# Graph outputs and first feed-forward chunk: order of loads, clears, rows and splits changed

## The reference

```python
# graph attention, h = 4 heads; x is layer-normed
alpha = einsum(q[dst], k[src]) / sqrt(512); attn = softmax over the edges of dst
agg = segment_sum(attn * v[src], dst)
x_attn = agg + x @ Wskip + bskip
h = x_attn @ Wlin + blin + x_attn[:, :512]
x1 = x + gamma * (h - mean(h)) / sqrt(var(h) + 1e-5) + beta
# feed-forward on xf = layernorm(x1), e = 4 experts
weights = normalised(max(softmax(xf @ gate_w.T) - sigmoid(xf @ thr_w.T) / e, 0))
hidden = relu(einsum('ni,ehi->neh', xf, fc1_w))
lo = (hidden @ lora_A) @ lora_B; x2 = x1 + sum_e weights * (lo @ fc2_w)
# used later: the sum of edge_attr (64 columns) and the count of edges per dst
```

## Time and profile before

| what | value |
|---|---|
| device time, median of 3 | 1934.83 us (1934.49 to 1940.91) |
| the profiled execution's own time | 1933.92 us |
| its span | 1932.3 us |
| granted TensorE clock, mean | 0.963 |
| PE busy | 1773.4 us, 92% |
| DVE busy | 1309.0 us, 68% |
| ACT busy | 909.0 us, 47% |
| POOL busy | 587.7 us, 30% |
| output loop | about 759 to 943 us |
| first chunk | 957 to about 1040 us |

### The profile page before, as it was taken

The page is one execution under the profiler, slowest core; times in us unless marked ns, Lnnn a source line. Parts: engine busy times, 40 slices in busy tenths (PEclk is TensorE's granted clock), DMA queues, the critical chain, the costliest instruction groups (busy, mean ns, idle before and its releaser), DMA issues. The chain is left out here.

```text
span 1932.3 us, 31958 instructions
## 1 busy us (share of the span) xinstructions
PE 1773.4 (92%) x10958; PEld 1542.0 (80%) x10958; DVE 1309.0 (68%) x2957; ACT 909.0 (47%) x1655; POOL 587.7 (30%) x532
## 2 busy tenths in 40 slices
PE   7998999899999999888679999999899999999496
PEld 5776899788888888776568998988788888888385
DVE  5444466788888886466764566545588788886676
ACT  4332366677777775222231233324465555555321
POOL 0000102655555551001100112122254535443234
PEclk9999999899999999998889999999999999999698
DMA  6752677877777774656213038876021111203432
GB/s 242 215 187 83 201 257 247 224 204 198 203 202 202 204 201 122 162 126 157 84 49 110 1 110 149 203 214 194 11 43 23 43 32 32 43 23 125 155 121 88
DMA packets 183532, 265.14 MB, mean 137 GB/s; under 512 B 55852, under 2 KB 102443, under 8 KB 181109
## 3 DMA queue, kind: packets, MB, share of 16 engines
q1 hardware_dynamic: 117839, 169.58, 30.1%
q0 software_dynamic: 49920, 62.94, 12.2%
q10 hardware_dynamic: 15640, 30.90, 6.5%
HBM read 198.55 MB, written 85.86 MB: 147 GB/s over the span
## 5 line engine op out<-in xcount | busy, mean ns | idle before, releaser
L1092 POOL DMA_INDIRECT edge_rows<-xn_store,edge_index x200 | 242.5, 1213 | 170.1 <-PE psum L138 108.5
L2599 POOL TENSOR_TENSOR mprob<-mprob,mrden 125x1250 f32<-125x1250 f32 x80 | 181.6, 2271 | 219.6 <-DVE mrden L2705 219.1
L2628 ACT ACTIVATE mprob<-psum,mbias 125x1250 f32<-125x1250 f32 x80 | 104.3, 1303 | 152.4 <-DVE mbias L2714 152.4
L1310 DVE TENSOR_TENSOR edge_xt_lo<-psum,edge_xt_hi 128x500 fp32r<-128x500 f32 x200 | 134.8, 675 | 56.3 <-ACT edge_xt_hi L1185 56.3
L1185 ACT ACTIVATE edge_xt_hi<-psum 128x500 fp32r<-128x500 f32 x200 | 117.5, 589 | 91.6 <-PE psum L1485 91.6
L2712 DVE TENSOR_REDUCE mmin<-psum 125x1 f32<-125x512 f32 (+1 forms) x240 | 126.9, 584 | 46.6 <-PE psum L2871 46.3
L2889 PE MATMUL psum<-ident,mprob 125*125 125x125 f32 x800 | 117.9, 292 | 17.9 <-DVE ptm_lo L2719 9.8
L2889 PEld LDWEIGHTS psum<-ident,mprob 125*125 125x125 f32 x800 | 100.3, 191 | 35.5 <-DVE ptm_lo L2719 20.4
L2719 DVE TENSOR_TENSOR ptm_lo<-psum,ptm_hi 125x500 fp32r<-125x500 f32 (+1 forms) x240 | 126.4, 582 | 2.0 <-ACT ptm_hi L2634 2.0
L1485 PE MATMUL psum<-ident,edge_rows 125*128 125x125 f32 x800 | 119.7, 273 | 4.8 <-DVE edge_xt_lo L1310 2.5
L1339 DVE TENSOR_TENSOR edge_rows_lo<-edge_rows,edge_rows_hi 125x1024 fp32r<-125x1024 f32 x100 | 121.2, 1212 | 0.0
(11 more groups left out here) (519 smaller groups left out, 5364.1 us busy)
## 6 DMA issues: line engine op xcount, KB each, us to landing
slots_in<-blank_rows ACTq DMA_DIRECT2D x20, 1026.0 KB, 16.8
t_store<-t_part SPq DMA_DIRECT2D x20, 1000.0 KB, 5.4
t_row<-t_store SPq DMA_DIRECT2D x47, 400.0 KB, 6.8
y_store<-y_rows SPq DMA_DIRECT2D x50, 200.0 KB
q_chunk<-q_store SPq DMA_DIRECT2D x40, 250.0 KB, 5.6
y_tile<-y_store SPq DMA_DIRECT2D x10, 896.0 KB
edge_attr<-in_attr SPq DMA_DIRECT2D x50, 112.0 KB
moe_xg<-slots_in SPq DMA_DIRECT2D x17, 256.5 KB, 3.6
```

The costliest lines, as they stand in the source:

```text
L1092: nc.gpsimd.indirect_dma_start(xe[t % RING][:, s, :], None, g.xn_store, bass.IndirectOffsetOnAxis(ap=index[t % RING][:, s, 0:1], axis=0)). ...
L1310: nc.vector.tensor_tensor(xt_lo[:, k, :], x_bank(KT * t + k), f32(xt_hi[:, k, :]), ALU.subtract).then_inc(x_low, 1)
L2599: nc.gpsimd.tensor_tensor(prob[:, n % 4, :], prob[:, n % 4, :], rden[:, n % 4:n % 4 + 1].broadcast_to([P, N]), ALU.mult).then_inc(p_ready, 1)
```

## The change

In the output loop: the first base rows, beta and the last rows of x are issued inside SP's loop (t = 0 and t = 6) behind the edge features, and the wait for the y stores goes; `fin.xin` is loaded at step 9 instead of 5, and POOL adds beta 4 windows later, so that those windows' clears stand ahead of it; `bound`, `turn_f` and `pass_ranges` are written in turn 38; some semaphores (`turn_inner`) are cleared ahead of the wait for `pass_done`. `scale` also writes `shift2`, minus mean times scale. In the first chunk: ACT writes rows 4 to 7 from `shift2` and `r2`; POOL's first clear waits for the four rows of DVE; the last pair's results follow its centring, with each later step one place earlier; ACT splits expert 3's weights behind `first_hi(8)` and `first_hi(9)`; DVE's `b_pads` comes earlier and its part of that split between the gates' spans; PE takes `second(0)` ahead of the last turns and the gates.

```diff
...
@@ -689,10 +689,12 @@
                                   [x[:, k, a:b] for x in xt], k == 0, k == KT - 1)
             last.then_inc(self.wide, 1)
 
-    def vector_rows(self, nc, dve):
+    def vector_rows(self, nc, dve, between=None):
         for q, (a, b) in enumerate(SPANS):
             dve.wait_ge(self.wide, q + 1)
             last = nc.vector.tensor_copy(self.rows[:, a:b], self.core.bank(q)[0:self.ROWS, 0:b - a])
+            if between is not None and q + 1 < len(SPANS):
+                between(q)
...
+        self.shift2 = at("fin_shift2", [P, NT], F32, 3.75)
...
     def scale(self, nc, link, c):
 
         rough_root(nc, link, self.r0[:], self.ve[:], self.h[:], (12.0, 768.0))
-        link(nc.vector.tensor_scalar(self.r2[:, 2 * c:2 * c + 2], self.r0[:], ROOT_SCALE, None, ALU.mult))
+        pair = slice(2 * c, 2 * c + 2)
+        link(nc.vector.tensor_scalar(self.r2[:, pair], self.r0[:], ROOT_SCALE, None, ALU.mult))
+        return nc.vector.scalar_tensor_tensor(self.shift2[:, pair], self.mv2[:, pair, 0], -1.0, self.r2[:, pair], ALU.mult, ALU.mult)
...
-    edge_inner, inner = [], []
+    edge_inner, turn_inner, inner = [], [], []
...
+    def turn_sem(name):
+        turn_inner.append(sem(name))
+        return turn_inner[-1]
+
...
-    attr_in, attr_top, attr_low = [loop_sem(f"attr_in{i}") for i in range(ATTRS)], loop_sem("attr_top"), loop_sem("attr_low")
-    hot_clear, hot_ready, agg_done, agg_out = (loop_sem(n) for n in ("hot_clear", "hot_ready", "agg_done", "agg_out"))
+    attr_in, attr_top, attr_low = [turn_sem(f"attr_in{i}") for i in range(ATTRS)], turn_sem("attr_top"), loop_sem("attr_low")
+    hot_clear, hot_ready, agg_done, agg_out = (turn_sem("hot_clear"), *(loop_sem(n) for n in ("hot_ready", "agg_done", "agg_out")))
...
 
@@ -1022,17 +1031,17 @@
                     if t == 1:
                         y_load(1)
                 y_store(WINDOWS - 1)
-                sp.dma_start(fin.beta[:], row_view(w["beta"])).then_inc(xin_in, 16)
-                in_two(sp, fin.last_xin[:], pair(w["x"], FIN), xin_in)
-                for i in range(2):
-                    sp.wait_ge(y_stored[i], 16 * (WINDOWS // 2))
-                in_two(sp, g.acc[:, 0:2, :], pair(g.base_store, 0), base_in)
                 for t in range(WINDOWS):
                     if t + RING < WINDOWS:
                         sp.wait_ge(hot_ready, t + 1)
                         firsts.append(index_load(sp, t + RING, index_in[t % RING]))
                     if t + ATTRS < WINDOWS:
                         attr_load(t + ATTRS, firsts[t + ATTRS])
+                    if t == 0:
+                        in_two(sp, g.acc[:, 0:2, :], pair(g.base_store, 0), base_in)
+                    if t == 6:
+                        sp.dma_start(fin.beta[:], row_view(w["beta"])).then_inc(xin_in, 16)
+                        in_two(sp, fin.last_xin[:], pair(w["x"], FIN), xin_in)
                     if t == 3:
                         for s in edge_inner:
                             sp.sem_clear(s)
@@ -1049,12 +1058,14 @@
                     if step == 1 and c:
                         sp.wait_ge(o_added, 2 * c)
                         in_two(sp, pair(g.base_store, c - 1), g.acc[:, 2 * c - 2:2 * c, :], base_out)
-                    if step == 5 and c < FIN:
+                    if step == 9 and c < FIN:
                         if c:
                             sp.wait_ge(xin_used, 2 * c)
                         in_two(sp, fin.xin[:], pair(w["x"], c), xin_in)
                 sp.wait_ge(o_added, NT)
                 in_two(sp, pair(g.base_store, FIN), g.acc[:, 2 * FIN:, :], base_out)
+                for s in turn_inner:
+                    sp.sem_clear(s)
                 sp.wait_ge(pass_done, 4 * turn + 4)
                 sp.sem_inc(pass_over, 1)
                 for s in inner:
@@ -1132,8 +1143,8 @@
                     nc.gpsimd.memset(f32(hot[i][:]), 0.0).then_inc(hot_clear, 1)
                 for t in range(WINDOWS):
                     clear(t)
-                    c, step = divmod(t, 2 * PER_TILE)
-                    if step == 9 and c < FIN:
+                    c, step = divmod(t - 4, 2 * PER_TILE)
+                    if step == 9 and 0 <= c < FIN:
                         pool.wait_ge(xin_in, 32 * c + 16 + 64)
                         nc.gpsimd.tensor_tensor(fin.xin[:], fin.xin[:], bc(fin.beta[:], 2), ALU.add).then_inc(xin_ready, 1)
                 nc.gpsimd.tensor_tensor(fin.last_xin[:], fin.last_xin[:], bc(fin.beta[:], 2), ALU.add).then_inc(xin_ready, 1)
...
                 if step == 15:
-                    fin.scale(nc, link, c)
+                    link(fin.scale(nc, link, c))
...
@@ -1442,11 +1453,12 @@
                     if h == 0 and r:
                         add_out(r - 1)
                         edge_sums(r - 1)
+                    if n == TURNS - 2:
+                        nc.vector.tensor_copy(bound[:], nb[:])
+                        link(nc.vector.tensor_scalar(g.turn_f[:], g.turn_f[:], 1.0, None, ALU.add))
+                        link(g.pass_ranges(nc, link))
                     for c in range(FIN):
                         finish(c, n - 2 * HEADS * c)
-                nc.vector.tensor_copy(bound[:], nb[:])
-                link(nc.vector.tensor_scalar(g.turn_f[:], g.turn_f[:], 1.0, None, ALU.add))
-                link(g.pass_ranges(nc, link))
                 add_out(NT - 1)
                 edge_sums(NT - 1)
                 g.pass_flags(nc).then_inc(pass_done, 1)
...
-    all_xs, x_copied, fin_done = sem("ffn_xs"), sem("ffn_x_copied"), sem("fin_done")
+    all_xs, late_xs, x_copied, fin_done = sem("ffn_xs"), sem("ffn_late_xs"), sem("ffn_x_copied"), sem("fin_done")
...
         @block.gpsimd
         def _(pool):
             link = core.pool_steps.on(pool)
+            pool.wait_ge(all_xs, 4)
             nc.gpsimd.memset(f32(a_both[:]), 0.0).then_inc(pads, 1)
             thin.gpsimd(nc)
             pool.wait_ge(fin_done, 2)
...
+            for t in range(4, 8):
+                nc.scalar.activation(xs[:, t, :], g.acc[:, t, :], ACT.Identity, bias=fin.shift2[:, t:t + 1],
+                                     scale=fin.r2[:, t:t + 1]).then_inc(late_xs, 1)
             for t in range(2):
                 first_hi(t)
...
@@ -1897,13 +1913,9 @@
                             copy_x(4 + m)
                         if c == 0 and e == 1:
                             if m == 0:
-                                act.wait_ge(all_xs, 8)
+                                act.wait_ge(late_xs, 4)
                                 act.wait_ge(x_copied, 8)
                             top(fc1_hi[2], fc1_raw[2], fc1_in[2], fc1_h[2], m)
-                        if c == 0 and e == 2 and m:
-                            if m == 1:
-                                act.wait_ge(fin_done, 2)
-                            top(fc1_hi[3], fc1_raw[3], fc1_in[3], fc1_h[3], m - 1)
...
                     if c == 0 and e == 2:
-                        top(fc1_hi[3], fc1_raw[3], fc1_in[3], fc1_h[3], KT - 1)
                         for t in range(8, NT):
                             first_hi(t)
+                        act.wait_ge(fin_done, 2)
+                        for k in range(KT):
+                            top(fc1_hi[3], fc1_raw[3], fc1_in[3], fc1_h[3], k)
                     if c == 0 and e == 3:
                         edge_tops()
                         gate_exponentials()
...
             def first_normal_row(t):
-                own = g.acc if t < 8 else x
+                own = g.acc if t < 4 else x
                 nc.vector.tensor_scalar(xs[:, t, :], own[:, t, :], fin.mv2[:, t, 0:1], fin.r2[:, t:t + 1],
                                         ALU.subtract, ALU.mult).then_inc(all_xs, 1)
...
             for t in range(4):
                 first_normal_row(t)
-            first_lo(0), first_lo(1)
-            for t in range(4, 8):
-                first_normal_row(t)
-            for t in range(2, 6):
+            for t in range(6):
                 first_lo(t)
...
@@ -2133,18 +2144,19 @@
                                 fin.second_root(nc, link)
                             if m == 3:
                                 fin.centred(nc, link, last_pair)
+                                for s in range(2):
+                                    fin.result(nc, last_pair, s, x).then_inc(fin_done, 1)
                         if c == 0 and e == 2:
                             if m == 0:
-                                for s in range(2):
-                                    fin.result(nc, last_pair, s, x).then_inc(fin_done, 1)
-                            if m == 1:
                                 dve.wait_ge(fin_done, 2)
                                 fin.spread(nc, link, last_pair, x)
+                            if m == 1:
+                                fin.moments(nc, link, last_pair)
                             if m == 2:
-                                fin.moments(nc, link, last_pair)
```

(15 more changed lines are left out.)

8 lines of the change are left out of this document (4 added, 4 removed).

## The result

| | before | after |
|---|---|---|
| device time, median of the first comparison | 1935.27 us (1934.49 to 1940.91) | 1905.63 us (1898.35 to 1911.92) |
| ratio, with its 95% interval | | 0.984 (0.982 to 0.986) |
| the profiled execution, its span | 1933.92 us, 1932.3 us | 1898.35 us, 1896.7 us |
| granted TensorE clock, mean | 0.963 | 0.972 |

The kernel is faster by 29.6 us, where 35.0 were forecast. The changed kernel was measured two more times, beside new runs of the kernel before: 30.1 us (1911.16 against 1941.24) and 34.6 us (1901.68 against 1936.31). The profiled pair differs by 35.6 us. The profiled run of after is the fastest of its four runs, so the medians are the fairer measure.

A forecast was written before the change was run, and what follows sets the result against it. TensorE (PE) was taken as the bound, losing 33.2 us to stalls and low clock in the output loop. Loop 28.3 + chunk start 0.7 + middle 6.0 = 35.0 us off 1933.9; with 0.9 for the median, 1899.8 us; range 1892.5 to 1909.

The forecast's parts named there:

- (a): Output loop: edge features issued ahead of beta, last x rows and accumulator rows; 9.3 us stall shrinks to 0 to 1.5.
- (b): Output loop: fin_x issued at step 9, added 4 windows later; 23.1 us of later stalls go to near 0.
- hardly waits: Sign that the forecast is right: in the output loop POOL hardly waits for fin_x.
- (c): Output loop: SP nearly the bound, some loads and a store late; 4.2 us of new small stalls (bounds 0, 9.3).
- the first stall: Output loop around 781 us: 9.3 us lost, as window 4's edge features were issued only at 776.74.
- the end's 0.75: End of the output loop: about 0.75 us lost where PE waits for a last yt_lo; it stays.
- Rival 1: Output loop: SP or transfers become the bound, attr loads late every tile; 13.5 us for the 4.2, 1909; chance 0.11.
- (d): Output loop: POOL's four adds beside busy DVE cost nothing, hidden by yt_lo's lead; 8.7 us if that lead is gone.
- (e): End of the graph stage: moving bound, turn_f, pass_ranges to head 38 and clearing semaphores early gains 0 (bounds 0, 1.5).
- (f): First chunk's start: DVE's rows without the memset beside them, rows 4 to 7 on ACT; 0.7 us (bounds 0, 1.8).
- (g): First chunk's middle: PE resumes at 994.3 instead of 999.26, gates at full clock; 6.0 us (bounds 3, 7.5).
- The 1.9 us for the clock in second(0): First chunk's middle: 1.9 us added to second(0)'s 3.6 us for the clock.

## Why the prediction was right, and where not

**Sign, size and bound: right.** PE's pace was the thing to read. The loop lost 33.2 us, and 25.3 came back (forecast 28.3, bounds 23 and 32.5). The outputs end at 918, not 914: 7.9 us of leftovers instead of 4.95, and 0.3 more at the start.

**(a), 9.3 to 0-1.5: the step that failed.** The wait itself went from 6.9 to 1.98 us, but with the low clock behind it 4.15 us stayed. Window 4's features were to be issued at 770.5 and in at 773.5; they were issued at 771.32 and in at 775.4, with the accumulator's rows issued 0.9 us behind them (with those rows a window later, and the y store behind the load, the landing took 2.25 us). The upper bound of 1.5 was set without the clock, which the prediction had counted in the 9.3. And (a) had a price of its own that the sum did not have: the last rows of x, moved to window 6, share the semaphore of POOL's first add. Alone, (a) gave 0, on top of (b) 3 to 4 us.

**(b), 23.1 to near 0: right in effect, 21.3 measured by itself.** "Neither POOL nor SP holds anything" was wrong as a sentence. POOL still stood 23.5 us for fin_x where "hardly waits" was said: it runs ahead of PE by the one-hot buffers, so 4 windows on its queue are not 12 us of time before it gets there, and the load took 5.9 to 6.5 us and not 4.3 (10.3 in the kernel with one DMA per window). Three of the four waits stay inside the lead; the first does not always.

**(c), 4.2: right in size, if the first stall is booked apart.** With the end's 0.75, 4.95 us were left in the sum; 7.9 were measured, 4.15 of them at the first stall and 3.8 for all the rest: a y_tile late, fin_x of the first pair late, half a microsecond in some tiles, 0.6 at the end. These are the kinds that (c) named. Rival 1 does not hold: from 840 on, tiles take 15.06 to 15.7 us.

**(d): right** in that the 8.7 us are not there, by the adds cut down. **(e): right,** the time between loop and chunk is 15.8 to 16.1 in all profiles.

**(f), 0.7, and (g), 6.0: 6.7 against 8.0** (7.5 to 8.8 over the profiles of after). PE resumed 36.0 us after DVE's first row (968.67 - 932.67); the forecast's 994.3 less 0.7 is 36.2. The gates took 7.2 us (7.0), at a granted 1.00. The 1.9 us for the clock in second(0) were a toss: it ran 3.67 us at 1.00 in four profiles with this chunk (all three of after among them), and 5.28 and 5.37 us at 0.69 and 0.68 in two, whose chunk gained 5.9 to 6.6 us, just the forecast. That the profiles of after beat it by 1.3 us is luck with the clock. And the order that the sum counted as part of the gain is worth less than none: second(0) behind the gates is 1 to 2 us better, since it waits for b_pads, the last thing that DVE makes there. (f) was costed a little low: POOL's wait alone is worth 1.1 to 1.5 us.

**The sum.** The two errors nearly cancel: -3.0 in the loop, +1.3 in the chunk leave 33.2 of 35.0 us; that they cancel is luck. The two changed stages gain 32.5 to 33.3 us in all three profiles of after, so the medians of 29.6, 30.1 and 34.6 must differ by the other stages or by the runs that no profile shows; which, is not shown. My first explanation for the missing 5 us, new stalls in the loop that fall differently from run to run, fell: the loop is 157.3 to 159.1 us in seven profiles that have the whole graph part and load the features in halves at the change's place. Up to the loop it is 759.0 and 759.7 in the profiles of before and 759.3 to 765.0 in those of changed kernels, and message passing is 125.8 to 128.0 in the four profiles on one chip, 121 to 123 in the others. Whether a changed kernel is a little later by rule at the loop, as these numbers suggest, stays open; two profiles of before are too few.

## What to carry to other kernels

Before you move a load back, look up who waits on its semaphore and what else is counted there: a shared semaphore makes the first to need it wait for the last to land. Parts of a change are priced one on top of the other, not one by one, since one part can make harmless what another delays. Price what is left of a stall with the clock behind it, not by the wait alone. Give an in-order queue's wait the lead of that queue, not the pace of the slowest engine, and a load's time from the busy stretch, not from a quiet one. When two jobs can go first on the bound engine, the first should be the one whose input is made first.

## What was not expected of the hardware

A load of 0.5 MB (fin_x, two halves) took 4.3 us from issue to use in a quiet stretch and 10.3 us behind a y_tile, with a DMA share of 0.71; 5.9 to 6.5 in the kernel after. A DVE tensor_scalar with one SBUF operand took 4.15 us for four rows beside GpSimd's memsets (938.16 to 941.2 us), and 1.92 us with the memset behind it, though the memset only writes. And the clock behind a short wait went either way: in the kernel after 0.64 behind 1.98 us at 776, 1.00 behind 1.45 us at 805 and behind 2.32 us at 968. Ahead of second(0), with the same code, waits of 2.31 or 2.32 us had 1.00 behind them in four profiles, and waits of 2.21 and 1.99 us 0.69 and 0.68 in two. The low level cost 1.6 to 1.7 us there, nearly as much as the wait.
